# Expert results weighted on ScalarE and added to the output by accumulating DMAs

## The reference

```
logits = x @ w_gate.T ;  p = softmax(logits)
p, chosen = top_k(p, 2) ;  p = p / sum(p)
for e in 8 experts:
    h   = silu(x @ w1[e].T) * (x @ w3[e].T)         # 704 wide
    out = out + (h @ w2[e].T) * (p of e, 0 if not chosen)
x = x + out                                          # x before the block: the residual
```

## Time and profile before

| | |
|---|---|
| median of 3 runs | 648.99 us (648.83 to 649.03) |
| the profiled execution | 644.79 us, its span 642.9 us |
| PE busy | 511.0 us (79%) |
| DVE, ACT, POOL busy | 418.6, 369.9, 149.9 us |
| expert steps (first fetch issued to last scatter landed) | 454.1 to 629.4 us |
| end stage (reload, sums, stores) | 629.4 to 642.9 us |

### The profile page before, as it was taken

How to read it: one execution, slowest core, us unless ns; L and a number is a source line. 1 busy time by engine, 2 the same in 40 slices (tenths; PEclk the granted TensorE clock), 3 DMA queues, 4 the chain that set the end, 5 groups by cost and what they waited for, 6 DMA issues and landing times.

```text
span 642.9 us, 14120 instructions
## 1 busy us (share of the span) xinstructions
PE 511.0 (79%) x5748; PEld 375.8 (58%) x5748; DVE 418.6 (65%) x629; ACT 369.9 (58%) x810; POOL 149.9 (23%) x115
## 2 busy tenths in 40 slices
PE   0287898877687765579979999996499999999980
PEld 0154565755466732354654565576499999995560
DVE  7989989999996678988985867758411111112224
ACT  7996888887898318557677666683512222222212
POOL 1000000000010137712218777320203222222110
PEclk9995599697977989899998999997799999999995
DMA  8700000000010000000000000000699999889816
GB/s 331 232 1 1 1 2 1 2 1 1 2 34 2 1 0 2 1 1 2 2 3 3 3 3 2 3 5 33 203 410 418 422 395 328 330 314 333 341 58 204
DMA packets 18191, 71.16 MB, mean 111 GB/s; under 512 B 4688, under 2 KB 9552, under 8 KB 14544
## 3 DMA queue, kind: packets, MB, share of 16 engines
q1 hardware_dynamic: 14976, 63.97, 26.1%
q0 software_dynamic: 1920, 5.25, 2.4%
q10 hardware_dynamic: 1232, 1.06, 0.5%
HBM read 65.55 MB, written 4.72 MB: 109 GB/s over the span
## 4 chain that ended last, share of the span: by engine, by line
PE 48%; DVE 35%; ACT 10%; issue 4%; DMA 2%; POOL 1%; DVEq 0%; ACTq 0%; POOLq 0%
PE PS L1524 29%; DVE arena L984 4%; DVE arena L1245 4%; DVE arena L977 4%; DVE nmx L1080 3%; PE PS L2058 2%; PE PS L1859 2%; PE PS L2127 2%; PE PS L1608 2%; PE PS L1589 1%; ACT arena L622 1%; PE PS L1876 1%; DVE arena L999 1%; DVE R L1006 1%; DVE arena L998 1%
## 5 line engine op out<-in xcount | busy, mean ns | idle before, releaser
L1524 PE MATMUL PS<-arena 128*128 128x128 f32 (+5 forms) x1360 | 147.0, 286 | 16.9 <-DVE arena L1180 11.5
L1524 PEld LDWEIGHTS PS<-arena 128*128 128x128 f32 (+3 forms) x1360 | 122.6, 162 | 40.8 <-issue 24.2
L622 ACT ACTIVATE arena<-PS,nmx 128x128 f32<-128x128 f32 (+1 forms) x128 | 52.3, 431 | 23.7 <-DVE nmx L1080 23.7
L1472 DVE TENSOR_TENSOR R<-arena,PS 128x128 f32<-128x128 f32 x16 | 4.6, 288 | 87.7 <-ACT arena L894 87.7
L489 POOL DMA_INDIRECT ypair<-arena,oid x20 | 19.8, 988 | 122.1 <-ACT arena L900 122.1
L392 POOL TENSOR_SCALAR arena<-ident,gcol 128x128 f32<-128x128 f32 x4 | 3.5, 890 | 187.6 <-DMA gcol<-in_gcol 187.6
L1589 PE MATMUL PS<-arena 32*128 32x128 f32 (+1 forms) x128 | 24.5, 467 | 28.0 <-ACT arena L622 28.0
L1524 PE MATMUL PS<-arena,R 128*128 128x256 f32 x192 | 44.2, 380 | 0.6 <-ACT arena L900 0.6
L454 POOL TENSOR_TENSOR arena<-arena 128x1024 f32<-128x1024 f32 x16 | 37.6, 2368 | 21.9 <-DVE arena L1293 21.9
L1524 PEld LDWEIGHTS PS<-arena,R 128*128 128x128 f32 x192 | 35.2, 190 | 5.1 <-issue 1.0
L984 DVE TENSOR_TENSOR_SCAN arena<-dmat,arena 128x1023 f32<-128x1023 f32 x16 | 37.6, 2348 | 0.6
(11 more groups left out here) (318 smaller groups left out, 1174.9 us busy)
## 6 DMA issues: line engine op xcount, KB each, us to landing
arena<-in_moe SPq DMA_DIRECT2D x23, 1408.0 KB, 8.0
arena<-in_moe SPq DMA_DIRECT2D x23, 768.0 KB, 9.3
inproj<-in_inproj SPq DMA_DIRECT2D x1, 1344.0 KB, 10.4
arena<-in_fT SPq DMA_DIRECT2D x2, 512.0 KB, 4.2
R<-in_w1T SPq DMA_DIRECT2D x1, 1024.0 KB, 6.6
R<-in_w2T SPq DMA_DIRECT2D x1, 1024.0 KB, 8.6
R<-in_w3T SPq DMA_DIRECT2D x1, 1024.0 KB, 10.6
xT<-in_xT SPq DMA_DIRECT2D x1, 1024.0 KB, 12.6
```

The costliest lines, as they stand in the source:

```text
L622: sc.activation(pr[u % 2][:, j, 0:n], PS[:, 2 * (u % 2) + j // 2, (j % 2) * 256:(j % 2) * 256 + n], ACT.Exp, bias=nmx[:, u % 2, j:j + 1], ...
L1524: last = mm(dst, l, r, start=(n == 0), stop=(n == len(pairs) - 1))
```

## The change

The output tensor grows by 128 spare rows, and becomes the place of summation. Behind fetch 1, SP stores the residual `xtok` into `out` (1024 KB, and 128 KB into the spare rows), and the weights `wt` into a DRAM table `wtab` (one float per place). POOL gathers each step's 128 weights from it into a column of `wrow`; ACT's copy of the down product multiplies by this column. POOL then adds the 128 rows into `out` by an indirect DMA that adds to what stands in the destination (`compute_op=ALU.add`). A token's two places may be in different steps, so each add waits until all earlier adds have landed. A two step can hold one token twice, so it is added in two DMAs of 64 useful rows each, the other half going to spare rows. The second is issued after the next gathers.

The order of the steps becomes 12 whole, 3 two, 1 one, 4 whole. DVE computes the indices `wid`, `addid` and `addtwo` once. The reload of `ypair`, its multiplications and sums and the stores at the end are gone.

```
-STEPS = [("whole", b) for b in range(15)] + [("two", 16), ("two", 17), ("two", 18), ("one", 19), ("whole", 15)]
+STEPS = [("whole", b) for b in range(12)] + [("two", 16), ("two", 17), ("two", 18), ("one", 19)] + [("whole", b) for b in range(12, 16)]
+ADDS = [sum(2 if kind == "two" else 1 for kind, b in STEPS[:s]) for s in range(BLK + 1)]
...
@@ SP, in the loop over fetches and behind it
-            sp.wait_ge(st_y, 16 * BLK)
-            for q in range(4):
-                sp.dma_start(y01[:, 0, 2 * q:2 * q + 2, :], rows_of(0, q)).then_inc(ld_y[q], 16)
-            for i in range(0, NT, 2):
-                sp.wait_ge(S["dve_out"], i // 2 + 1)
-                sp.dma_start(out[P * i:P * (i + 2), :].rearrange("(i p) n -> p i n", p=P), xtok[:, i:i + 2, :])\
-                    .then_inc(st_out, 16)
-            sp.wait_ge(st_out, 16 * NT // 2)
+                if n == 1:
+                    sp.wait_ge(S["act_xtok"], 4)
+                    sp.dma_start(wtab.rearrange("(p w) n -> p (w n)", p=P), wt[:].rearrange("p s i -> p (s i)")).then_inc(st_w, 16)
+                    sp.dma_start(out[0:N, :].rearrange("(i p) n -> p i n", p=P), xtok[:]).then_inc(st_out, 16)
+                    sp.dma_start(out[N:N + P, :], xtok[:, 0, :]).then_inc(st_out, 16)
+            sp.wait_ge(st_out, 32)
+            sp.wait_ge(st_y, 16 * ADDS[BLK])
...
@@ POOL, behind the first four gathers
+            def gather_weights(s):
+                b = STEPS[s][1]
+                pool.indirect_dma_start(wrow[:, b:b + 1], None, wtab,
+                                        bass.IndirectOffsetOnAxis(ap=wid[:, b:b + 1], axis=0)).then_inc(ld_w[s % XR], 16)
+
+            def add_rows(s, n, index):
+                if ADDS[s] + n:
+                    pool.wait_ge(st_y, 16 * (ADDS[s] + n))
+                pool.indirect_dma_start(out, bass.IndirectOffsetOnAxis(ap=index, axis=0),
+                                        yb[s % YB], None, compute_op=ALU.add).then_inc(st_y, 16)
+
             pool.wait_ge(S["dve_gid"], 2)
+            pool.wait_ge(st_w, 16)
+            for s in range(XR):
+                gather_weights(s)
+            pool.wait_ge(S["dve_gid"], 3)
+            pool.wait_ge(st_out, 32)
             for s in range(BLK):
-                b = STEPS[s][1]
+                kind, b = STEPS[s]
                 pool.wait_ge(S["act_y"], s + 1)
-                pool.indirect_dma_start(ypair, bass.IndirectOffsetOnAxis(ap=oid[:, b:b + 1], axis=0),
-                                        yb[s % YB], None).then_inc(st_y, 16)
+                if kind == "two":
+                    add_rows(s, 0, addtwo[:, 0, b - 16:b - 15])
+                else:
+                    add_rows(s, 0, addid[:, b:b + 1])
                 if s + XR < BLK:
                     gather(s + XR)
+                    gather_weights(s + XR)
+                if kind == "two":
+                    add_rows(s, 1, addtwo[:, 1, b - 16:b - 15])
...
@@ ACT, result(b)
                 act.wait_ge(S["pe_y"], b + 1)
+                act.wait_ge(ld_w[b % XR], 16 * (b // XR + 1))
                 if b >= YB:
-                    act.wait_ge(st_y, 16 * (b - YB + 1))
-                sc.activation(yb[b % YB], bank(7, 256), ACT.Copy).then_inc(S["act_y"], 1)
+                    act.wait_ge(st_y, 16 * ADDS[b - YB + 1])
+                sc.activation(yb[b % YB], bank(7, 256), ACT.Copy, scale=wrow[:, n:n + 1]).then_inc(S["act_y"], 1)
...
-            for i in range(NT):
-                if i % 2 == 0:
-                    act.wait_ge(ld_y[i // 2], 32)
-                sc.activation(yw[:, i, :], y01[:, 1, i, :], ACT.Copy, scale=wt[:, 1, i:i + 1]).then_inc(S["act_yw"], 1)
```

More of the change, by code:

```diff
@@ L49, with build @@
 MAGIC = 1.5 * 2.0 ** 23
-def build(nc, a, arow, ypair, out):
+def build(nc, a, arow, wtab, out):
     F = mybir.dt.float32
@@ L247, in build @@
         pcol = sb("pcol", [P, 1])
-        padrow = sb("padrow", [P, BLK])
+        padcol = sb("padcol", [P, 4])
         ub = sb("ub", [P, P], BF)
@@ L274, in build @@
         spare = sb("spare", [P, BLK])
-        oid = sb("oid", [P, BLK], U32)
         gid = sb("gid", [P, BLK], U32)
+        addid = sb("addid", [P, BLK], U32)
+        addtwo = sb("addtwo", [P, 2, 3], U32)
+        pastpad = sb("pastpad", [P, 3])
+        wid, wpart = (sb(n, [P, BLK], U32) for n in ("wid", "wpart"))
+        wrow = sb("wrow", [P, BLK])
         PS = ctx.enter_context(nc.psum_tensor("PS", [P, 8, HALF], F))
@@ L288, in build @@
         ld_dn = [sem(f"ld_dn{i}") for i in range(RING)]
-        ld_y = [sem(f"ld_y{i}") for i in range(4)]
+        ld_w = [sem(f"ld_w{i}") for i in range(XR)]
         st_row = sem("st_row")
+        st_w = sem("st_w")
         st_y = sem("st_y")
@@ L312, in chained @@
             return done
-        def rows_of(s, q):
-            return ypair[N * s + 2 * P * q:N * s + 2 * P * (q + 1), :].rearrange("(i p) n -> p i n", p=P)
         block = ctx.enter_context(nc.Block())
@@ L343, in _ @@
             for n, m in (("uiota", uiota), ("within_of", within_of), ("again", again), ("iop", iop), ("pcol", pcol),
-                         ("padrow", padrow)):
+                         ("padcol", padcol)):
                 load(m[:], a[n], "route")
@@ L909, in _ @@
             result(BLK - 1)
-            act.wait_ge(st_y, 16 * BLK)
-            for q in range(4):
-                act.dma_start(y01[:, 1, 2 * q:2 * q + 2, :], rows_of(1, q)).then_inc(ld_y[q], 16)
-            for i in range(NT):
-                if i % 2 == 0:
-                    act.wait_ge(ld_y[i // 2], 32)
-                sc.activation(yw[:, i, :], y01[:, 1, i, :], ACT.Copy, scale=wt[:, 1, i:i + 1]).then_inc(S["act_yw"], 1)
         @block.vector
@@ L1445, in tokens_of_blocks, with result_rows @@
                 done(v.tensor_scalar(gid[:], ids[:], N - 1, None, ALU.bitwise_and), "dve_gid")
-                done(v.scalar_tensor_tensor(spare[:], ids[:], float(OUT), padrow[:], ALU.is_equal, ALU.mult))
-                done(v.tensor_tensor(oid[:], ids[:], spare[:], ALU.add), "dve_gid")
+            def result_rows():
+                done(v.tensor_scalar(wpart[:], ids[:], P - 1, None, ALU.bitwise_and))
+                done(v.tensor_scalar(wid[:], ids[:], 7, None, ALU.logical_shift_right))
+                done(v.tensor_scalar(wid[:], wid[:], 2 * NT - 1, None, ALU.bitwise_and))
+                done(v.scalar_tensor_tensor(wid[:], wpart[:], float(2 * NT), wid[:], ALU.mult, ALU.add), "dve_gid")
+                done(v.tensor_scalar(spare[:], ids[:], float(OUT), padcol[:, 0:1], ALU.is_equal, ALU.mult))
+                done(v.tensor_tensor(addid[:], gid[:], spare[:], ALU.add))
+                done(v.tensor_scalar(pastpad[:], addid[:, 16:19], padcol[:, 1:2], None, ALU.add))
+                for l in range(2):
+                    done(v.tensor_scalar(addtwo[:, l, :], pastpad[:], padcol[:, 2 + l:3 + l], padcol[:, 0:1], ALU.mult, ALU.add),
+                         "dve_gid" if l else "dve_self")
             top_values(0)
@@ L1462, in _ @@
             tokens_of_blocks()
+            result_rows()
             def hidden_block(s):
@@ L1506, in _ @@
                 hidden_block(s)
[L1508 to L1515, removed]
         @block.tensor
@@ L2221, in arrange @@
     o["pcol"] = np.arange(P, dtype=f4).reshape(P, 1)
-    o["padrow"] = np.ascontiguousarray(np.arange(BLK * P, dtype=f4).reshape(BLK, P).T)
+    slot = np.arange(P)
+    o["padcol"] = np.stack([N + slot, -N - slot, slot < UNIT, slot >= UNIT], 1).astype(f4)
     r = np.arange(P)
@@ L2241, in program @@
             for n, v in arrays.items()}
-    out = nc.dram_tensor("out_0", (N, D), mybir.dt.float32, kind="ExternalOutput").ap()
+    out = nc.dram_tensor("out_0", (N + P, D), mybir.dt.float32, kind="ExternalOutput").ap()
     arow = nc.dram_tensor("arow", (N, D), mybir.dt.float32, kind="Internal").ap()
-    ypair = nc.dram_tensor("ypair", (OUT + BLK * P, D), mybir.dt.float32, kind="Internal").ap()
-    build(nc, args, arow, ypair, out)
+    wtab = nc.dram_tensor("wtab", (OUT, 1), mybir.dt.float32, kind="Internal").ap()
+    build(nc, args, arow, wtab, out)
 def kernel(**inputs):
@@ L2256 @@
     r = run_bass_kernel_spmd(nc, [{"in_" + n: v for n, v in arrays.items()}], core_ids=[0])
-    got = r.results[0]["out_0"]
+    got = r.results[0]["out_0"][0:N]
     return np.ascontiguousarray(got).reshape(B, T, D)
```

7 lines of the change are left out of this document (3 added, 4 removed).

## The result

The changed kernel took 659.67 us (median of 5 runs, 655.7 to 662.14), the kernel before 648.83 on the same chip (5 runs, 644.07 to 649.03): ratio 1.0197, 95% interval 1.0162 to 1.0232. (The ratio is not the quotient of the two medians, which is 1.0167.) It is slower, and above the predicted range of 638 to 658. The profiled execution took 655.7 us, the fastest of the five; its span is 653.9, 11.0 more than the span before.

The account below looks back on a forecast made before the run. PE was taken to set the pace, with the DMA engines about as full at first. End stage -13.3, last adds +0.6 and chained adds +5.6 gave -7.1: span 635.8, execution 637.7, forecast 642.0 us; 8-in-10 range 638 to 658.

Parts of the forecast that it names:

- Chained adds beside fetches: Expert steps: each add waits for the one before, 7.5 us to landing; PE stalls on late gathers, together +5.6.
- My 1.6 for another 128 KB: Gather behind a scatter: 128 KB more in the queue cost 1.6 us; half of that was added for an add's read.
- rival A: Early steps and two steps: adds pace them; at 10.2 us per add +3.3, 652.3 us; chance 0.36.
- C's second sum: Change only pays for itself: adds of 7.5, 2.6 stall at step 2, slow last adds +7, giving 649; chance 0.07.
- Whole steps: Whole steps: an add of 7.5 plus about 0.2 wake-up just fits into 7.72 us, so counted 0.
- margin of 3.5: Gathers behind waiting adds: an add may be 3.5 us late before PE stalls.
- Two steps: Two steps: adds don't fit, so PE stalls 2.6 and then 3.0 us for gathers; together +5.6.
- Last adds: End of the kernel: a quiet add takes 3.0 us, no wait between the last two; +0.6.
- End stage: End of the kernel: removing reload, sums and last store saves 13.5 us, less 0.2 for SP's wait and block end; -13.3.
- Stores, weights, indices, scaling, order: Residual stores before fetch 2, weight gathers, index computation, ACT's scaled copy and new step order: each counted 0.
- The skill's rule: Adds beside fetches: half a copy's rate would double 6.7 to 13.4 us, a clear loss; set against the change.

Follow-up runs that it names:

- e2: The changed kernel with the adding transfers replaced by plain scatters, all waits kept, sums left out; 642.64 us, ratio 0.9908.
- h1: The kernel before with gathered weights applied in ACT's copy, ACT's end multiplications gone, last quarter's sums on POOL; 649.53 us, ratio 1.0039.
- g4: The changed kernel with one add per step, each into rows of its own, so no add waits for another; sums left out; 639.12 us, single run.
- f4: The changed kernel without the gathers of weights, every result scaled by 0.5; 656.11 us, single run.
- e3: The changed kernel with the order of steps of the kernel before; 654.77 us, ratio 1.0118.
- e1: The changed kernel with POOL issuing the gather of step s+4 ahead of the waiting add of step s; 657.74 us, ratio 1.0144.
- f1: The changed kernel with each fetch cut by columns into 4 + 2 narrower transfers; 654.09 us, ratio 1.0135.
- f2: The changed kernel with each fetch cut into 4 + 2 transfers and the gather issued ahead of the waiting add; 649.43 us, ratio 1.0048.
- f3: The kernel before with each fetch cut into 4 + 2 narrower transfers, as a control; 646.72 us, ratio 1.0005.
- g3: The changed kernel with only the first of the two adds of each two step; 645.46 us, single run.

## Why the prediction was wrong, point by point

- **The step that failed: "Chained adds beside fetches".** The mechanism was named rightly (POOL waits for an add, the gather behind it is late, PE stalls), the link was sized at 7.5 plus 0.2. It measured 8.8 to 10.8 plus 0.8 where the DMA was full and in the two steps, 5.8 to 8.1 between. Over the window of the earlier trace rows its median is 6.4: the value was about right for the middle and wrong where it decides. My 1.6 for another 128 KB priced bytes; the add sends four times the packets. This is rival A, which was said to decide from 9.0, and A's sign, PE waiting for gathers in the early steps, came.
- *Sums of the rivals:* by the prediction's own steps the two steps cost 5.6 at 9.0 per add (the gather behind step 13's first add lands at 602.2), not 8, so A at 9.0 would still have gained some 1.6; C's second sum gives 651, not 649. This changes nothing in the account.
- *Whole steps, counted 0:* the margin of 3.5 was eaten by the second step. Three waits, 6.2 us; rival A had 6.5. From 522 us on the links fitted again, as the forecast had it.
- *Two steps, counted 5.6:* one wait of 9.8 in place of two (rival A: 8.0), and 2.4 more as PE came back at the lower clock, which no rival counted.
- *Last adds, counted +0.6:* a quiet add takes 3.8, not 3.0. With the wake-up that made 4.4 from issue to issue (642.50 to 646.91), more than the 3.5 between the last two results (3.39 before), so the last add waited for the one before after all: 0.8 + 0.9.
- *End stage, counted -13.3:* the 0.2 for the end of the block was wrong. SP's wait at the end, after and before, reads

```profile
SPq L62 <- PEq L62: 2.9, 1, 2.9
```

```profile
SPq L61 <- PEq L61: 0.2, 1, 0.2
```

  After the last add has landed (650.7), 2.9 us more go by until POOL is done. The profile names PE, but the last engine at work is POOL, whose last instruction (DRAIN) starts at 646.7 and takes 7.0. It reads as follows in the changed kernel, in the kernel before, in e2 and in h1, in turn:

```profile
L62 POOLq DRAIN  x1: 6988/6988/6988, 646.7 to 646.7; - x1
```

```profile
L61 POOLq DRAIN  x1: 4543/4543/4543, 626.8 to 626.8; - x1
```

```profile
L62 POOLq DRAIN  x1: 6422/6422/6422, 636.0 to 636.0; - x1
```

```profile
L61 POOLq DRAIN  x1: 6288/6288/6288, 640.3 to 640.3; - x1
```

  In the kernel before, POOL was done at 631.3, beside the end stage. In e2 and g4 the wait after the landing is 3.7 and 2.7. It is not the landing that sets this end: it comes 5.2 after POOL's last issue is over in the changed kernel and in e2 alike, though the copy lands some 1.3 sooner, and in h1 5.0 after POOL's last sum, when no scatter was in flight. So even without a chain the stretch from the last issue to the end is 6.7 (g4) in place of 15.9: a gain of 9, not of 13.
- *Stores, weights, indices, scaling, order:* 0 is about right for the first four. PE waited 0.6 for a fetch, once, at step 2, so the stores used up the margin there and a little more; f4 shows nothing, and in g4, which has all four, the stretch from the first gather to the last issue is 1.7 longer than before. The order was not 0: with chained adds it is worth 0.8%, some 5 us, by the ratios of e3 and of the changed kernel.
- *The skill's rule:* the prediction set the rule of "Collectives: The Full Stack" in the Trainium skill (half the rate for a reducing transfer) beside its rows. Alone, an add takes 3.8 where a scatter takes 2.4, a factor of 1.6; beside fetches, from 478 to 520 us, 9.3 where the scatter takes 6.6, 1.4. The rule overstates it, but its sign was the right one; whether the second read is the reason, no run shows.

That the profiled execution lies 7.6 above rival A's sum (+10.9 in place of +3.3) is mostly POOL's closing (2.7), the clock (2.4) and the longer wait in the two steps (1.8).

## What to carry to other kernels

A DMA that has to wait for the landing of the one before costs its full time to landing, plus 0.8 us of wake-up here, per link: compare that sum with the period of the step, at the fullest stretch of the DMA and not at its median, and count the links. If it doesn't fit, everything behind the waiting instruction on that queue is late, and putting that work ahead of the wait mostly moves the stall (from 16.0 to 14.0 us in e1); with links near the period it helped more (from 9.9 to 3.7 us, f1 to f2). An end stage that goes takes its cover along: see what else ended beside it, and what paces it (in h1 the loads, and POOL's own end).

## What the runs showed of the hardware that was not expected

- An accumulating indirect DMA of 128 rows of 1 KB sends 128 data packets, a plain one 32; POOL issues it in 1.6 us, the plain one in 1.0.
- Its time to landing fell with the length of the packets beside it: 9.3, 7.2 and 6.9 us beside fetch packets of 7.7, 2.6 and 1.4 KB; 3.8 alone. Plain scatters fell too, from 6.6 to 5.8 with the cut fetch (f3).
- POOL is done only 3.3 to 5.2 us after its last instruction is over, landed or not: 3.3 in the kernels that issue 40 DMAs on POOL (before, f3), 4.1 with 43 (f4), 5.0 with 60 (g3, g4, h1), 5.2 with 63 (the changed kernel, e2). So it rises with their number here; the reason is not shown. When nothing else covers it, the kernel ends that much later.
- After 9.8 us of idling PE worked at 0.50 of its clock for some 5 us.
